# A graph network and mixture-of-experts kernel: one 4608 KB weight load moves from SyncE's queue to ScalarE's, and VectorE's spectral chain waits for its DRAM round trip two subtractions later

## The reference

```python
v = jnp.clip(x @ v_w + v_b, -V_MAX, V_MAX)
a = (-2.0 + v).astype(jnp.complex64) - 1j
G = bk_green_diag(a)                       # two scans along the 625 nodes
feats = jnp.stack([G.real, G.imag], axis=-1)
probs = jax.nn.softmax(x @ gate_w + gate_b, axis=-1)
topv, topi = jax.lax.top_k(probs, K)       # 2 of 8 experts
comb = jnp.sum(topv[..., None] * jax.nn.one_hot(topi, E, dtype=x.dtype), axis=2)
h = jax.nn.gelu(jnp.einsum('bnd,edf->bnef', x, w1) + b1)
y = jnp.einsum('bnef,efd->bned', h, w2) + b2
ffn_out = jnp.einsum('bne,bned->bnd', comb, y)
return ffn_out + bk_scale * (jnp.clip(feats, -10., 10.) @ out_w + out_b)
```

## Time and profile before

| | us |
|---|---|
| median of three runs | 1468.29 |
| lowest and highest of the three | 1457.69, 1469.85 |
| the profiled execution, whole | 1451.72 |
| its span, first to last instruction | 1449.9 |
| PE busy in the span | 1313.8 (91%) |
| mean granted TensorE clock | 0.953 |

### The profile page before, as it was taken

How to read it: one execution, slowest core, us unless ns; L and a number is a source line. 1 busy time by engine, 2 the same in 40 slices (tenths; PEclk the granted TensorE clock), 3 DMA queues, 4 the chain that set the end, 5 groups by cost and what they waited for, 6 DMA issues and landing times.

```text
span 1449.9 us, 22872 instructions
## 1 busy us (share of the span) xinstructions
PE 1313.8 (91%) x7548; PEld 1096.0 (76%) x7548; DVE 956.5 (66%) x2154; ACT 553.2 (38%) x650; POOL 643.6 (44%) x569
## 2 busy tenths in 40 slices
PE   7988688889979979999999999999999889989991
PEld 5765688556976549999999999999967679556660
DVE  8967998877757255566566656565258975467664
ACT  1011566222310024545454545555248651223330
POOL 7025777777667633333333433343167730121102
PEclk9999788989989988999999999999999999999996
DMA  6960000020460226787878787878589862447635
GB/s 181 77 132 6 2 2 1 2 67 1 130 178 3 67 98 232 272 288 264 288 255 288 270 283 250 304 264 286 147 271 341 266 200 66 120 131 212 197 104 184
DMA packets 112660, 243.85 MB, mean 168 GB/s; under 512 B 30397, under 2 KB 52090, under 8 KB 112492
## 3 DMA queue, kind: packets, MB, share of 16 engines
q1 hardware_dynamic: 77628, 136.46, 31.7%
q0 software_dynamic: 22432, 72.27, 17.7%
q10 hardware_dynamic: 12528, 34.22, 6.1%
HBM read 202.05 MB, written 45.31 MB: 171 GB/s over the span
## 4 chain that ended last, share of the span: by engine, by line
PE 67%; DVE 18%; DMA 6%; ACT 3%; issue 2%; POOL 1%; ACTq 1%; DVEq 1%; SPq 0%; POOLq 0%
PE PS L2705 24%; PE PS L2662 5%; PE PS L2908 5%; PE PS L2388 4%; PE PS L2919 3%; PE PS L2764 3%; PE PS L2539 3%; PE PS L2695 3%; PE PS L2834 3%; PE PS L2592 2%; PE PS L2876 2%; DVE e L1318 2%; DMA raw<-in_L_gnn_W_rel 2%; DVE wlo L1318 2%; DVE e L1560 1%
## 5 line engine op out<-in xcount | busy, mean ns | idle before, releaser
L827 POOL DMA_INDIRECT xg<-xn_dram,xrow x70 | 116.2, 1659 | 305.1 <-DVEq L1527 273.5
L2705 PE MATMUL PS<-whi,xhi 128*128 128x384 f32 x840 | 221.2, 344 | 1.0 <-ACTq L1109 1.0
L2705 PE MATMUL PS<-whi,xlo 128*128 128x384 f32 x840 | 214.4, 336 | 0.0
L2705 PE MATMUL PS<-wlo,xhi 128*128 128x384 f32 x840 | 213.1, 335 | 0.0
L1318 DVE TENSOR_TENSOR wlo<-raw,whi 128x2304 fp32r<-128x2304 f32 x68 | 175.3, 2578 | 40.0 <-ACTq L1092 34.8
L1090 ACT ACTIVATE whi<-raw 128x2304 fp32r<-128x2304 f32 x68 | 145.1, 2134 | 20.0 <-DMA raw<-in_L_gnn_W_rel 11.2
L2705 PEld LDWEIGHTS PS<-wlo,xhi 128*128 128x128 f32 x840 | 152.2, 188 | 0.0
L2705 PEld LDWEIGHTS PS<-whi,xlo 128*128 128x128 f32 x840 | 151.6, 188 | 0.0
L2705 PEld LDWEIGHTS PS<-whi,xhi 128*128 128x128 f32 x840 | 148.2, 189 | 1.3 <-issue 1.3
L1318 DVE TENSOR_TENSOR xlo<-PS,xhi 128x768 fp32r<-128x768 f32 x70 | 67.0, 958 | 123.5 <-ACTq L1101 116.7
L795 POOL DMA_INDIRECT evwb<-inv_dram,idxb x80 | 108.6, 1358 | 30.6 <-issue 22.4
(11 more groups left out here) (452 smaller groups left out, 2584.6 us busy)
## 6 DMA issues: line engine op xcount, KB each, us to landing
raw<-in_L_gnn_W_rel SPq DMA_DIRECT2D x68, 1152.0 KB
z_dram<-xn ACTq DMA_DIRECT2D x70, 384.0 KB, 5.8
wroot<-in_L_ffn_w SPq DMA_DIRECT2D x12, 576.0 KB, 5.8
y_dram<-yb ACTq DMA_DIRECT2D x17, 384.0 KB, 3.5
pre<-in_L_ffn_w SPq DMA_DIRECT2D x9, 576.0 KB, 5.6
gw<-in_L_gnn_W SPq DMA_DIRECT2D x2, 2304.0 KB, 27.2
fw<-in_L_ffn_w SPq DMA_DIRECT2D x8, 576.0 KB, 5.0
fw<-in_L_ffn_w SPq DMA_DIRECT2D x1, 4608.0 KB, 21.9
```

What stands on the lines that cost most here:

```text
L827: pool.indirect_dma_start(xg[b][j][:, :], None, xn_dram, bass.IndirectOffsetOnAxis(ap=xrow[:, b, j:j + 1], axis=0)).then_inc(x_gathered[b] ...
L2705: mm = pe.matmul(slot(q)[:, s * BANK:s * BANK + HALF], a[:, k, :], wt[:, k, s * HALF:(s + 1) * HALF], start=(k == 0 and part == 0), stop=( ...
```

## The change

Three edits. The load of `fw2` is taken out of SyncE's list and issued by ScalarE, on ScalarE's own DMA queue, behind `gelus(1)` and `chunk_high(4)`. The chain gets one more `yield`, right behind the signal of `spec_ready`, so that signalling and waiting are now in two pieces; the number of pieces ahead of `chunk_low(7)` goes from 9 to 10, and takes the signal with it. And VectorE's loops are cut anew: behind `weigh_chunk(3)` come chunks 4 and 5 with `chunk_low(8)` and `chunk_low(9)` and no piece of the chain, and from chunk 6 on two pieces stand between `chunk_low(c + 4)` and `weigh_chunk(c)`.

```diff
@@ SyncE
             load_next_pair(3)
-            sp.dma_start(fw2[:, 0:FK, :], w["L0_ffn_w2"].rearrange("e f d -> (e f) d").rearrange("(c p) d -> p c d", p=128)).then_inc(ld_f2, 16)
             through_dram(2, mat_dram, S[:, BC:BC + 2, :].rearrange("p a b -> p (a b)"),
@@ ScalarE
                 gelus(c, c % 2, c // 2)
                 if c + 3 < FK:
                     chunk_high(c + 3)
+                if c == 1:
+                    act.wait_ge(layer_done, 1)
+                    act.dma_start(fw2[:, 0:FK, :], w["L0_ffn_w2"].rearrange("e f d -> (e f) d").rearrange("(c p) d -> p c d", p=128)).then_inc(ld_f2, 16)
@@ VectorE, spectral_steps
                 dve.sem_inc(spec_ready, 1)
+                yield
 
                 dve.wait_ge(spec_in, 32)
@@ VectorE
             for c in (5, 6, 7):
-                spectral_part(8 if c < 7 else BC - 16)
+                spectral_part(8 if c < 7 else BC + 1 - 16)
                 chunk_low(c)
-            for c in range(4):
+            for c in range(6):
+                if c >= 4:
+                    chunk_low(c + 4)
                 weigh_chunk(c)
-            spectral_part(1)
-            for c in range(4, FK):
+            for c in range(6, FK):
                 if c + 4 < FK:
                     chunk_low(c + 4)
+                spectral_part(2)
                 weigh_chunk(c)
-                spectral_part(2)
             for _ in spectral:
                 pass
```

## The result

The changed kernel takes **1452.07 us** (median of 20 runs, 1446.07 to 1460.25), the kernel before, on the same chip, 1463.87 (20 runs, 1455.08 to 1476.25). The ratio is 0.9931, with a 95% interval of 0.9913 to 0.9949. The ratio is worth 10.1 us, the two medians differ by 11.8. In us the interval is 7.5 to 12.7. That is under 1% and clear of noise. The forecast was 1456.4, 11.9 us less, within 1%. The 4.3 us between 1456.4 and 1452.07 are in the start of the sum: the median of three runs that it began from, 1468.29, was 4.4 us above the median of twenty.

The account below looks back on a forecast made before the run. PE was taken as the bound, waiting 10.14 us for VectorE between chunks 7 and 8. Removing 10.3 us of stall and 1.56 of low clock, with nothing added, gives 1468.3 - 11.9 = 1456.4 us, range 1446 to 1466.

Parts of the forecast that it names:

- The stall and the clock: PE between chunks 7 and 8: 10.3 us of standing still and 1.56 of low clock removed, together 11.9 us.
- Chunk 8 to 11 in time: VectorE's subtractions of chunks 8 to 11 come before PE wants them, with 5.1, 7.4, 7.5 and 6.0 us spare.
- What the transfer costs its neighbours: Loads beside fw2 keep 297 GB/s, taking 26.3 us; the mat_dram write is held only a few packets; PE loses nothing.
- my two bounds of 297 and 206: GB/s beside fw2: 297 taken, pair 3 by 406.4; at 206, by 418.1, 4.1 us gained, 1464 us, chance 0.13.
- ScalarE is not held: ScalarE's issue of fw2 after chunk_high(4) fits its 2.41 us of idle time and costs nothing.
- The rival in which it is held: ScalarE held 15.9 us by issuing fw2, gelu 2 and chunk 4 late: only 3.1 us gained, 1465 us, chance 0.04.
- the third rival: Behind the block, GpSimd's scatters end over 9 us later and delay the first gather: 1462 at 15 late, chance 0.07.
- Slower: The write behind pair 3 and ml land late, ahead of chunk_low(11), and PE idles: 1478 us, chance 0.04.

Follow-up runs that it names:

- e7: The changed kernel once more, no edit, for a second profile: 1451.99 us.
- e10: The changed kernel as it is, no edit, timed beside the kernels with held loads: 1451.31 us, ratio 0.9935 to the kernel before.
- e4: The changed kernel with ScalarE issuing fw2 three gelus later, behind gelu 4 and the high part of chunk 7: 1452.54 us, ratio 0.9914 to before.
- e9: The changed kernel with e4's later load, and SyncE's raw loads held until the second scatter batch has landed: 1452.29 us, ratio 0.9931 to before.
- e6: The kernel before, VectorE's order kept, with fw2 issued by ScalarE behind gelu 4 and the high part of chunk 7: 1461.92 us, ratio 0.9991.
- e1: The load alone: fw2 issued by ScalarE as in the change, SyncE's and VectorE's orders those of before: 1460.01 us, ratio 0.9973 to before.
- e8: The changed kernel with SyncE's raw loads for the next block held until the second scatter batch has landed: 1452.70 us, ratio 0.9936 to before.
- e2: The order alone: VectorE's order and extra yield as in the change, fw2 issued by SyncE as before: 1456.83 us, ratio 0.9939 to before.
- e5: The changed kernel with PE doing only 8 of the 12 hidden chunks in the outer phase, result not the reference's: 1450.25 us, ratio 0.9905 to before.
- e3: The kernel before once more, no edit, for a second profile: 1462.98 us.

## Why the prediction was right, and where it was not

**The stall and the clock: right.** The step said 10.3 us of standing still and 1.56 of low clock. After has no wait at chunk 8, its first group takes 1.93 us, and the stretch from chunk 1 to the outer phase is 10.9 us shorter over five profiles, with 11.9 said. The 1.0 that is missing is a matter of the term's size. The forecast took PE's 10.14 us from one execution. In the second one, which had waited ahead of chunk 3, the stall was 6.65, and part of what the change frees is in such executions spent on that earlier wait. Counted from chunk 3 it is 10.1, since the earlier wait lies outside this count and the shorter stall inside. That the ratio gives 10.1 too is chance: its interval goes from 7.5 to 12.7.

**Chunk 8 to 11 in time: right, with far less spare than said.** The spare times were given as 5.1, 7.4, 7.5 and 6.0 us. In after they were 0.6, 2.6, 5.7 and 4.1. Chunk 8's subtraction was done at 402.96 and PE wanted it at 403.60; in e7 and e10 there were 0.65 and 0.55 us. That is what the late read of `vch` took: it stands ahead of the subtraction of chunk 5, and chunks 6, 7 and 8 then follow with 0.5 to 0.7 us to spare. With `fw2` issued later chunk 8 has 4.4 us (e4) and 5.0 (e9), near the 5.1 of the forecast. So that the sum held was close, and in part luck: before the change chunk 5 had 4.5 us to spare, `vch` took about that much and 0.3 to 1 us more, and each further us of it would have been a us of PE. Chunk 9's subtraction was done at 406.26, and PE wanted it at 408.86. There the cause is pair 3, for which ScalarE waits 5.05 us; I had allowed 2. Pair 3 was issued 25.0 us after chunk 1's start, 3.7 later than in before, since the write of `comb_dram` ahead of it took 3.7 us longer.

**What the transfer costs its neighbours: the step that failed in part.** It said that beside `fw2` the bytes would move at 297 GB/s, and that by packet turns `fw2` on its own queue could not hold the small write longer than a few packets. The traces show three things in its place. From the issue of `fw2` to the start of chunk 9's high part the rate was 252 GB/s, between my two bounds of 297 and 206, and the stretch took 31.4 us where I had 26.3. The small write took 5.2 us beside a large load on another queue (e6), 5.3 in e4 and 5.8 in e9, against 1.3 without one (e1). So the rule of the Trainium skill, "DMA: Bandwidth & Descriptors", Queues, rings and completion order, holds in direction here, as the write is done 4 us before the load in e6, while in the load's own queue it was done only with it (in before the load landed at about 413.0, and the read that waits for the write was issued at 413.25); the size that I read from it does not hold. And two neighbours were not in the sum at all. One is the write of `comb_dram`: 4.9 to 6.8 us in the six profiles in which `fw2` is issued behind gelu 1, 1.7 to 2.6 in the six others. The other is the read of `vch`, issued 3.5 us behind `fw2`, for which VectorE waits 4.70, 5.62 and 4.64 us in the three profiles of the changed kernel and not at all in before or e4. It stands ahead of the subtraction of chunk 5, and there PE waits 0.29, 0.84 and 0.96 us (1.07 in e8, whose block is the same). I had priced the chunks from 8 on only, though the load starts while chunk 2 is on its way. It cost PE about 1 us at the most, so the sum stood.

**Which half does it: not said, and the prediction's words credit both.** The first paragraph says that both ends of the wait are touched. The runs divide it: the order alone gives 0.9939 with no wait on PE, the load alone 0.9973 with the wait still there, and a load moved to the other queue but met in flight 0.9991. VectorE's order is the cause; the transfer's move on top of it adds, if anything, less than these intervals can tell. The wait for the round trip moved behind three subtractions, those of chunks 8, 9 and 10, one more than the title says. What the Trainium skill says under "DMA: Bandwidth & Descriptors", Issuing engines are not separate DMA queues, by which no bandwidth is won and the gain has to come from the order, agrees with this: the rate was 252 GB/s after and 297 before, and e2 has nearly the whole gain without the move.

**ScalarE is not held: right.** The issue took it 0.45 us, and its idle time there was 1.75. The rival in which it is held is out.

**Behind the block: the third rival was in part at work.** I had said 9 us between the end of the scatters and the gather's call. After has none left, and lost 0.8 us; e7 lost about 3; e8, with SyncE's next loads held back, has 8 us left, and e10, without a hold, 16. So the margin goes the way that the rival named, by transfers that meet the scatters, except that it was the loads of `raw` and not `fw2` that met them. It does not decide, as it takes 0 to 3 us of 11. e5 shows that it would decide the next such change: of 25.8 us less on PE only 2 to 4 are in the time.

**Slower: out.** The write behind pair 3 took 6.9, 6.7 and 5.8 us in the changed kernel's three profiles, `ml` was there before VectorE asked for it, and PE never waited for chunk 11.

**Left open.** Whether e4 is a true 2 us better than the change (0.9914 against 0.9931 and 0.9935, with overlapping intervals) was not settled. No version here beats the change clearly.

## What to carry to other kernels

When an engine waits for a transfer ahead of work that another engine is waiting for, first put that work ahead of the wait; it cost nothing here and held even when the small write took 15.9 us (e2), while a faster transfer cures only as much as it becomes faster. When a large load is moved to another queue, list every small transfer that is issued while it is in flight, from its first us on and not only those at the old stall, and allow each of them some 4 us more, which is what the small transfers took here. Then look at the spare time of every step behind them and not only at the waits: here it fell from 5 us to 0.6 without a wait to show for it. And profile the kernel before twice: one stage or one stall may be 3 to 8 us off in the one execution that a sum is made from.

## What the runs showed of the hardware that I had not expected

A 1.6 KB write took 1.3 us with hardly a load in flight (e1), 5.2 to 5.8 us with 4608 KB in flight on another engine's queue (e6, e4, e9), and 7.4 to 15.9 us behind them in its own (e3, before, e2), where it was done 20.6 to 23.0 us after the issue of the large load whenever it was issued itself. The issue of the same 4608 KB kept SyncE for 2.17 us in two profiles, for 0.71 in a third, and ScalarE for 0.45 in all nine in which it had it. SyncE's two loads of pair 3 kept it for 3.6 to 5.8 us in the six profiles in which `fw2` had been issued ahead of them on the other queue, and for 1.0 to 1.3 us in the six others. I read this as a filled queue that holds the engine which issues to it; no run here tests that. What is shown is that everything behind such an issue on the same engine starts later.
